# Graph attention over a sparse 8192 x 8192 adjacency: loading the matrix in 2 MB pieces of 128 rows by 4096 columns instead of 1 MB pieces of 128 by 2048

## What is computed

```python
h  = relu(layernorm(x)) @ W                      # 8192 x 128
e  = leaky_relu((h @ a_src)[:, None] + (h @ a_dst)[None, :], 0.2)
e  = where(adj > 0, e, -9e15)
out = x + softmax(e, axis=1) @ h
```

## Time and profile before

| | |
|---|---|
| median of three runs | 843.11 us (842.23 to 843.27) |
| the profiled execution | 841.73 us, of which the span of its instructions is 839.9 us |
| busy: DVE, POOL, ACT, PE | 71%, 67%, 65%, 65% of the span |
| data read and written | 307.97 MB and 8.59 MB, 377 GB/s over the span |
| loads of `adj` | 256 of 1 MB, 21.1 us from issue to landing (median) |
| mean granted clock of TensorE | 0.64 of full speed |

### The profile page before, as it was taken

How to read it: one execution, slowest core, us unless ns; L and a number is a source line. 1 busy time by engine, 2 the same in 40 slices (tenths; PEclk the granted TensorE clock), 3 DMA queues, 4 the chain that set the end, 5 groups by cost and what they waited for, 6 DMA issues and landing times.

```text
span 839.9 us, 8878 instructions
## 1 busy us (share of the span) xinstructions
PE 545.6 (65%) x1847; PEld 237.8 (28%) x1847; DVE 599.7 (71%) x2790; ACT 547.4 (65%) x374; POOL 559.8 (67%) x575
## 2 busy tenths in 40 slices
PE   4757677677676676666776655767677667666231
PEld 3642122233232222322332222323233222223231
DVE  7905457676776778876777768788797676779983
ACT  3969767767676676767676676676767666676000
POOL 3723777776677667676676775777777767767760
PEclk9889655655555666666556667665655665666555
DMA  9999999999999999999999999999999999993110
GB/s 285 419 300 316 398 398 398 400 398 401 402 402 400 403 402 402 403 400 403 401 403 400 401 401 403 398 389 396 393 391 402 392 399 383 391 396 119 31 26 5
DMA packets 75014, 299.21 MB, mean 356 GB/s; under 512 B 14986, under 2 KB 36274, under 8 KB 42192
## 3 DMA queue, kind: packets, MB, share of 16 engines
q1 hardware_dynamic: 49248, 276.84, 83.7%
q0 software_dynamic: 17024, 17.48, 6.7%
q10 hardware_dynamic: 8688, 4.33, 2.8%
HBM read 307.97 MB, written 8.59 MB: 377 GB/s over the span
## 4 chain that ended last, share of the span: by engine, by line
DMA 74%; ACT 11%; DVE 8%; issue 3%; PE 2%; SPq 1%; ACTq 0%; POOLq 0%; DVEq 0%
DMA adj_buf<-in_adj 74%; ACT mask_buf L423 9%; DVE x_all L718 3%; SPq L236 1%; ACT work L388 1%; PE banks L943 1%; PE banks L912 1%; ACT gathered L403 0%; ACT work L398 0%; DVE x_all L714 0%; PE banks L902 0%; DVE rest L578 0%; DVE words L580 0%; DVE words L576 0%; ACTq L415 0%
## 5 line engine op out<-in xcount | busy, mean ns | idle before, releaser
L327 POOL DMA_INDIRECT gathered<-table,index x512 | 510.5, 997 | 217.0 <-issue 171.5
L423 ACT ACTIVATE mask_buf<-adj_buf,minus_half 128x2048 bf16<-128x2048 int32 x256 | 511.4, 2001 | 210.9 <-DMA adj_buf<-in_adj 209.3
L943 PE MATMUL banks<-mask_buf,bit_ident 128*128 128x512 bf16 x1024 | 414.1, 552 | 147.6 <-ACT mask_buf L423 146.8
L943 PEld LDWEIGHTS banks<-mask_buf,bit_ident 128*128 128x128 bf16 x1024 | 105.3, 124 | 369.4 <-ACT mask_buf L423 225.7
L718 DVE SCALAR_TENSOR_TENSOR x_all<-gathered,weight,x_all 128x128 f32<-128x128 f32 x512 | 158.2, 349 | 9.3
L576 DVE MAX8 words<-banks 128x8 f32<-128x512 f32 x64 | 44.5, 696 | 156.3 <-PE banks L943 156.3
L941 PE MATMUL banks<-key_rows,ones_b 3*128 3x512 bf16 x64 | 33.7, 527 | 62.3 <-ACT mask_buf L423 61.8
L982 PE MATMUL banks<-x_all,one_hot 128*128 128x128 f32 x128 | 40.4, 415 | 13.8 <-DVE x_all L718 13.8
L580 DVE MAX8 words<-rest 128x8 f32<-128x512 f32 x64 | 44.5, 695 | 2.2
L311 POOL TENSOR_SCALAR work<-x_all,mv_all,rstd 128x128 f32<-128x128 f32 x32 | 27.0, 855 | 27.5 <-DVE nbias L535 13.8
L578 DVE MATCH_REPLACE8 rest<-words,banks 128x512 f32<-128x512 f32 x64 | 43.6, 681 | 0.0
(11 more groups left out here) (144 smaller groups left out, 487.6 us busy)
## 6 DMA issues: line engine op xcount, KB each, us to landing
adj_buf<-in_adj SPq DMA_DIRECT2D x256, 1024.0 KB, 21.1
gathered<-table,index POOLq DMA_INDIRECT x512, 2.5
table<-gathered ACTq DMA_DIRECT2D x4, 1040.0 KB, 15.7
out<-x_all SPq DMA_DIRECT2D x31, 128.0 KB
x_all<-in_x SPq DMA_DIRECT2D x2, 512.0 KB, 5.2
w_gathered<-table,w_index POOLq DMA_INDIRECT x16, 3.9
out<-x_all SPq DMA_DIRECT2D x2, 64.0 KB
w_ext<-in_L_gnn_W ACTq DMA_DIRECT2D x1, 64.0 KB, 3.3
```

What stands on the lines that cost most here:

```text
L327: nc.gpsimd.indirect_dma_start(g_view[buf][:, b, k, :], None, table, bass.IndirectOffsetOnAxis(index[:, buf, b, k:k + 1], 0), bounds_check ...
L423: nc.scalar.activation(mask_buf[:, u], adj_buf[:, u], ACT.Sign, bias=minus_half[:]).then_inc(mask_ready, 1)
L943: ins = mm(bank, bit_ident[:, h * PART_BITS + c], mask_buf[:, u, c * BIT_COLS:(c + 1) * BIT_COLS], start=False, stop=(h == PARTS - 1 and c ...
```

## The change

A load takes two neighbouring units at once: 128 rows by 4096 columns, 2 MB, 16 KB in one run from each row, into two neighbouring places of `adj_buf`. There are four loads per batch instead of eight, each with one semaphore. Both units of a pair wait for the same semaphore. SP issues the next load of a pair of places when both of their masks are made. Masks, matmuls and everything behind them stay per unit; the size of `adj_buf` stays.

```diff
+LOADS = UNITS // 2
...
-        adj_loaded = [sem(f"adj_loaded{u}") for u in range(UNITS)]
+        adj_loaded = [sem(f"adj_loaded{w}") for w in range(LOADS)]
...
-            def load_unit(i, u):
-                sp.dma_start(adj_buf[:, u, :], adj[bass.ds((i * BATCH + u // PARTS) * P, P),
-                                                   u % PARTS * PART:(u % PARTS + 1) * PART]).then_inc(adj_loaded[u], 16)
-
-            def load_batch(i, first=0, last=UNITS):
-                for u in range(first, last):
-
-                    sp.wait_ge(mask_ready, (i - 1) * UNITS + u + 1)
-                    load_unit(i, u)
+            def load_pair(i, w):
+                sp.dma_start(adj_buf[:, 2 * w:2 * w + 2, :].rearrange("p u n -> p (u n)"),
+                             adj[bass.ds((i * BATCH + 2 * w // PARTS) * P, P),
+                                 2 * w % PARTS * PART:(2 * w % PARTS + 2) * PART]).then_inc(adj_loaded[w], 16)
+
+            def load_batch(i):
+                for w in range(LOADS):
+
+                    sp.wait_ge(mask_ready, (i - 1) * UNITS + 2 * w + 2)
+                    load_pair(i, w)
...
-            for u in range(UNITS):
-                load_unit(0, u)
+            for w in range(LOADS):
+                load_pair(0, w)
...
             def mask(i, u):
-                act.wait_ge(adj_loaded[u], 16 * i + 16)
+                act.wait_ge(adj_loaded[u // 2], 16 * i + 16)
```

## The result

The changed kernel takes 838.81 us, the median of seven runs (835.98 to 840.69); the kernel before takes 842.99 (seven runs, 842.23 to 843.88). The ratio is 0.995, 95% interval 0.9934 to 0.9966: 4.2 us less, where 8.9 were forecast. The profiled execution is the fastest of the seven, 835.98 us, 2.8 under their median; its span is 834.2, 5.7 less than the span before.

A forecast was written before the change was run, and what follows sets the result against it. Loads by DMA were taken to bound the kernel, one or a few late engines pacing it. Terms -8.9 - 2.0 + 2.0 = -8.9 us from 843.1 gave 834.2 us; its own range 825 to 841.6, the overall range 826 to 849.

The forecast's parts named there:

- What bounds the kernel: Long stage: DMA loads of adj bound it; one or a few engines some 14 us behind set the pace.
- Part 1: Loads of adj up to unit 247: fewer, longer runs save 0.039 us per MB, -8.9 us over 230 units.
- rival 1: Loads of adj: the longer run saves nothing, only coarseness is left; 840 to 850.5 us, chance 0.17.
- rival 2: Each DMA engine's run: one of 16 KB costs more than two of 8 KB; slower, up to 1174 us, chance 0.08.
- rival 4: Each transfer has a fixed time that shows, at most 0.18 us; 22 us saved, about 821 us, chance 0.04.
- Part 2: Prologue: waiting for 2 MB against ACT let go sooner at the second table store; -2.0 us, between -4.8 and +5.4.
- Part 3: End of the loads: both masks of a pair follow its landing, +2.0 us; the same delay is covered in the long stage.
- Part 4: SP issue, out stores and gathers beside longer packets: no cost, gathers having about 26 us to spare.
- rival 3: Gathers starve beside 16 KB packets, needing three turns instead of two; slower, 1115 us, chance 0.04.
- No wait of DVE for a gather: Sign of the forecast being right: DVE would not wait for gathers, as in the long stage before.

The follow-up runs named there:

- first group: Runs on one chip of the changed kernel unedited, coarse_units, and pairs only in the first two or only in the later batches; kernel before there 844.93 us.
- coarse_units: Kernel before with 1 MB loads and 8 KB runs, but two loads issued and awaited together as in the change; 850.41 us, ratio 1.0055.
- pairs_again: The changed kernel run again with no edit; 840.31 us, ratio 0.9953 to the kernel before.
- early_pairs: The changed kernel with pairs in the first two batches only, single 1 MB loads after; 846.12 us, ratio 1.0014 to the kernel before.
- pairs_block_store: The changed kernel with table stores in 8320-byte blocks, gathers fetching wrong rows, for timing only; 829.57 us, ratio 0.9844 to the kernel before.
- block_before: Kernel before (1 MB loads) with table stores in 8320-byte blocks and DVE computing the new row numbers; 836.76 us, ratio 0.9926.
- third group: Runs on one chip with block table stores and right rows, with 1 MB, 2 MB or 4 MB loads; 828.17 to 836.76 us.

## Why the prediction was wrong

**What bounds the kernel: right.** ACT's waits in the long stage are for loads as before (193.0 us, all for `adj`), and the start of unit 247's mask orders the kernels of each group as their times do. That one or a few engines are last is seen after as before: from 758 us the DMA share is 0.24 and 0.15, while masks wait for loads until 767.08. Which engine it is and why stays open.

```profile
758.00:762.00 4.00, 2.15 (x14) 1.31 (x12) 3.69 (x20) 1.63 (x2) 2.99 (x3) 1.00 0.24 61
762.00:766.00 4.00, 2.44 (x11) 0.91 (x12) 3.83 (x13) 3.50 (x3) 2.99 (x3) 0.59 0.15 39
```

**Part 1, -8.9: right.** The fixed part was put at 8.6 ns per run. A 16 KB run took 615 ns, forecast 618. The saving per engine and unit was 0.038 us against 0.039, and the 230 units from unit 17 took 8.0 us less (2.857 us per MB, forecast 2.85). 8 us come out of the first group, 8.9 out of the third. So this term was 0 to 1 us too large, no more. This refutes rival 1 (nothing saved), rival 2 (a dearer run) and rival 4 (22 us from a fixed time per transfer): coarse_units has 256 transfers and the changed kernel 128, and all that lies between them is 10.1 us, where rival 4 had 22. The Trainium skill (DMA: Bandwidth & Descriptors, Anatomy of one DMA) fits 2.0 us fixed per transfer, and it does so for transfers that GpSimd issues; these loads come from SP, so the prediction leaned on it further than the page goes. No time of that size shows here, with three or more loads queued: even all of the 10.1 us would be 0.08 us for each of the 128 transfers saved.

**Part 2, -2.0: wrong, and this is the step that failed.** "With the stores drained sooner the pair starts at about 66 to 67." The first half was right: ACT is let go at once (0.69 us; forecast sooner than 47.4, at 45.4) and its masks come 1.4 us earlier. The second was not. The prediction took the pair to start 3 to 4 us before the load that the earlier trace rows show, and counted no rows for it. The queues of the changed kernel from 60 to 70 us:

```profile
q10 hardware_dynamic: 2987, 1.54, 114.7%
q1 hardware_dynamic: 18, 0.29, 13.7%
```

2987 rows are 187 per engine, 59 more than the last store has, at 10 us / 187 = 53 ns each and not 45. (Shares over 100% aren't only different queues side by side: from 62 to 68 us q10 alone has 123.8%. The 53 ns are time that passed per row, not the length of a row's record.) So the pair, issued at 62.83, doesn't move before 68, about when unit 13 did before, and it has one MB more to bring: it lands at 76.91, where a start at 66 to 67 gives some 72. The 512 rows per engine should have been held against the dry time: at 45 to 53 ns they are 23 to 27 us, and all of it has to fit between the loads up to 70.

Measured, unit 17 lands at 86.70 and not at 84: part 2 is **+0.7 us** and not -2.0, +1.7 in pairs_again, and early_pairs has +1.2 in all. The delay at 75 us is larger than that, 2.4 us, and one profile each doesn't fix it: from 30 to 75 us the three kernels that start with pairs load 8.27 to 9.01 MB, and the five that start with 1 MB loads and the old stores 9.06 to 9.89, 0.90 MB or 2.5 us more on average. All of these stay inside the ends given for part 2 (-4.8 to +5.4), but the value taken has the wrong sign. pairs_block_store shows the cause by taking it away: the late pair goes, and some 9 us with it. That is more than the 3 or 4 between -2.0 and what was measured, since the stores cost the kernel before too (block_before, -6.7 even with DVE's additional work). Why no run of the pair gets in between the rows for 5 us, where at 34 to 44 us the two queues went one for one, stays open.

**Part 3, +2.0: right in the profile** (1.9 us, the two masks behind the landing at 743.82), and in the account of the third group. Its other half, that the coarser landing is covered in the long stage, holds too (2.905 us per MB beside 2.904).

**Part 4, at nothing: half right.** I wrote that the gathers have some 26 us to spare and looked for starvation in the gathers themselves (rival 3). They were not starved: 460 gathers in the same 620 us. What starved was the `table` store that they wait for, by the very rule that I had read off: one row for each run of `adj`, whose length the change doubles. "No wait of DVE for a gather" was a sign of being right and failed: DVE waited 49.5 us. Its cost was nothing as far as tested (22 us of delay, not 32).

**The sum.** With what was measured for each part, -8.0 + 0.7 + 1.9 = -5.4 in the profiles. Of the 3.5 us that this lies over the forecast's -8.9, 2.7 are part 2 and 0.9 part 1. The medians differ by 4.2 only, since the profiled execution is 2.8 us under its median and that of the kernel before 1.3; where the changed kernel's wider scatter comes from stays open. Putting the 2.4 us of 75 us into the forecast's own sum would give -4.5 and look like a perfect account, but most of these 2.4 us are made good by unit 17.

## What to carry to other kernels

Queues of one DMA engine took turns here by the single run, not by bytes, once both were moving (533 rows beside 535 runs; 26 rows in 16 us beside runs of 0.615 us). But a load issued at 62.83 us behind queued rows moved nothing until 68. Before making the runs of one queue longer, list what shares the engines with it and comes in small pieces, add up all its pieces (not those of the last transfer), and ask who waits for the last one. Longer runs gained some 8 to 9 ns for each run saved on each engine; coarser issue and landing cost at the ends of a stream, where nothing covers them: use the long form in the middle and the fine one at both ends.

## What was unexpected of the hardware

- Four stores of 1040 KB to device memory took 50.9% of 45 us of the engines in 520-byte rows, and 22.6% in 8320-byte blocks. The gain from the stores' form (6.7 us in the kernel before) was larger than that from the loads' form.
- The last rows of a store drain at one per run beside a stream of 16 KB runs, whether they are left on one or two of 16 engines (61 rows from 76 to 100 us) or on about a dozen (455 in pairs_again): the store took 47.0 us to land. What decides how many engines are left with rows wasn't found out.
- From 120 to 740 us all 16 engines together moved 231.88 MB on q1 and 231.99 before, and yet the landings from unit 17 to unit 247 came 1.2% faster (2.857 and 2.892 us per MB). Only a part of this is the gathers' later place (3.0 us per engine); a load lands with the last engine, and that is not the mean one.
- A 32 KB run has 0.021 us per engine and MB less than a 16 KB run, which has 0.036 less than 8 KB: the fixed part holds over these three sizes.
